# Rotating the tile order of the second hop, running it two half steps ahead, and turning round the edge order of the second relation layer in a graph network kernel

## The reference, cut to what matters

```python
# block 3: two hops, then a product
for _ in range(K_HOPS):
    msg = segment_sum(norm[:, None] * h[src], dst)
    h = (1.0 - ALPHA) * msg + ALPHA * x
return relu(h) @ W.T + b
# block 4: two layers, each with 8 relations
xt = einsum('ni,rio->rno', x, W)             # 8 products of 256x256 for each node
msg = relu(xt[edge_type, src] + b)           # one row for each edge
return segment_sum(msg, dst)
```

## Time and profile before

| What | us |
|---|---|
| median of three executions | 2688.56 |
| the profiled execution, its own time | 2689.72 |
| its span, first to last instruction | 2687.9 |
| last hop-two tile done alone, first gather of layer one | 1507 to 1511 |
| last gather starts | 2675.07 |

### The profile page before, as it was taken

The page is one execution under the profiler, slowest core; times in us unless marked ns, Lnnn a source line. Parts: engine busy times, 40 slices in busy tenths (PEclk is TensorE's granted clock), DMA queues, the critical chain, the costliest instruction groups (busy, mean ns, idle before and its releaser), DMA issues.

```text
span 2687.9 us, 41486 instructions
## 1 busy us (share of the span) xinstructions
PE 2387.7 (89%) x11183; PEld 1798.7 (67%) x11184; DVE 1336.4 (50%) x2819; ACT 572.3 (21%) x1718; POOL 1620.1 (60%) x1701
## 2 busy tenths in 40 slices
PE   7799999999699999999999799998799798766666
PEld 4589999999456588888777477775455555544444
DVE  6788888888676721112373334443344334322232
ACT  1366666666000000000111101111122022000000
POOL 5777777720057777777100377664675757777776
PEclk9899999999799999999999999999899899887887
DMA  3033333322366688553443456653565455333443
GB/s 111 22 118 112 115 115 115 115 114 113 117 191 188 185 315 277 159 180 110 165 148 115 159 161 193 183 159 95 166 184 159 128 154 179 109 103 104 121 120 102
DMA packets 203201, 388.37 MB, mean 144 GB/s; under 512 B 52864, under 2 KB 136942, under 8 KB 202890
## 3 DMA queue, kind: packets, MB, share of 16 engines
q1 hardware_dynamic: 52356, 180.31, 20.0%
q0 software_dynamic: 66944, 111.48, 15.7%
q10 hardware_dynamic: 83718, 94.32, 10.3%
HBM read 244.89 MB, written 141.08 MB: 144 GB/s over the span
## 4 chain that ended last, share of the span: by engine, by line
PE 71%; DVE 10%; issue 8%; POOL 5%; DVEq 2%; ACT 2%; DMA 1%; PEldq 0%; SPq 0%; POOLq 0%; PEld 0%; ACTq 0%
PE agg L1045 16%; PE agg L1166 14%; PE y L922 13%; PE agg L986 9%; PE y L963 5%; POOL gathered L819 5%; PE y L1045 4%; PE agg L1041 4%; PE prod L907 2%; PE y L966 1%; DMA gathered<-table_rel,idx_rel 1%; ACT gathered L1295 1%; DVE onehot L1983 1%; PE y L865 1%; PE turn_ps L892 1%
## 5 line engine op out<-in xcount | busy, mean ns | idle before, releaser
L819 POOL DMA_INDIRECT gathered<-table_rel,idx_rel x840 | 809.4, 964 | 580.4 <-ACTq L1411 258.2
L1166 PE MATMUL agg<-gathered,onehot 128*128 x2072 | 577.3, 435 | 192.4 <-DVE onehot L1983 113.6
L1166 PEld LDWEIGHTS agg<-gathered,onehot 128*128 128x128 f32 x2072 | 434.6, 218 | 328.5 <-issue 262.8
L1983 DVE SCALAR_TENSOR_TENSOR onehot<-iota,keybase,edges 128x256 f32<-128x256 f32 x518 | 240.9, 484 | 642.7 <-PE agg L1166 542.5
L803 POOL DMA_INDIRECT edges_parted<-stream x416 | 402.3, 967 | 179.9 <-issue 126.5
L764 POOL DMA_INDIRECT edges_bucketed<-edges,stream x416 | 401.4, 965 | 148.7 <-issue 122.6
L986 PE MATMUL agg<-h_sb,stream 128*128 128x257 f32 x1250 | 334.9, 392 | 0.0
L1045 PE MATMUL agg<-gathered,stream 128*128 128x256 f32 x1250 | 271.7, 381 | 0.0
L1045 PEld LDWEIGHTS agg<-gathered,stream 128*128 128x128 f32 x1250 | 239.2, 191 | 32.6
L963 PE MATMUL y<-gathered,rel_sb 128*128 128x128 f32 x1300 | 234.8, 290 | 12.6 <-ACT gathered L1295 11.2
L963 PEld LDWEIGHTS y<-gathered,rel_sb 128*128 128x128 f32 x1300 | 218.2, 192 | 36.2 <-ACT gathered L1295 14.4
(11 more groups left out here) (209 smaller groups left out, 2405.3 us busy)
## 6 DMA issues: line engine op xcount, KB each, us to landing
table_rel<-rel_sb ACTq DMA_DIRECT2D x200, 256.0 KB, 3.1
stream<-weights_dense SPq DMA_DIRECT2D x41, 832.0 KB
stream<-weights_dense SPq DMA_DIRECT2D x41, 768.0 KB
weights_dense<-stream SPq DMA_DIRECT2D x25, 832.0 KB, 3.4
stream<-counts_dense SPq DMA_DIRECT2D x50, 416.0 KB
table_rel<-zeros ACTq DMA_DIRECT2D x16, 1280.0 KB
weights_dense<-stream SPq DMA_DIRECT2D x25, 768.0 KB, 3.2
stream<-counts_dense SPq DMA_DIRECT2D x50, 384.0 KB
```

Source lines behind the costliest of these rows:

```text
L819: pool.indirect_dma_start(gathered[:, slot * D:(slot + 1) * D], None, tables[n], bass.IndirectOffsetOnAxis(ap=idx_rel[:, c:c + 1], axis=0) ...
L1166: mm = pe.matmul(agg[b][:, 0:D], onehot[:, place * 2 + k, :], gathered[:, bass.ds(((p + pairs0) & (GP - 1)) * (2 * D) + k * D, D)], start= ...
L1983: nc.vector.scalar_tensor_tensor(onehot[:, place * 2:place * 2 + 2, :], iota[:].unsqueeze(1).broadcast_to([P, 2, P]), keybase[:, bass.ds(t ...
```

## The change

The second hop takes its tiles in the order 10 to 24, then 0 to 9 (`real_tile`); everything in it that reads a tile's block row, scale, rows or residual does so by the real number. So the 15 tiles that are done first are 10 to 24, and the edges of the first pass of layer one are those from tiles 10 to 24; `rel1b` takes those from tiles 0 to 9. Inside `rel1a` the half steps run two ahead: three of them in front of tile 0, then one for each tile.

Layer two takes the parts the other way round. `rel2a` has the edges from tiles 0 to 9, `rel2b` those from 10 to 24, so only ten layer-two products have to be made in `rel1b` (in front of tiles 3 to 12) and fifteen in `rel2a` (three ahead, then in front of tiles 1 to 12). For that, the parted edges are written twice, one copy behind the other, into a new DRAM tensor, and read back from an offset of `late` quads into `kept2`, in the space of the hop's first block row; a second list of indices and of bounds is worked out. POOL waits for that list before layer two. The zeroed rows are tiles 0 to 9 in table one (as many as before) and 10 to 24 in table two (15 instead of 10).

```diff
+    LATE = TILES - EARLY
...
-        def step_at(i):
-            return STEPS[(i + 1) // 2], (i + 1) % 2
+        def steps_with(t):
+            halves = range(3) if t == 0 else (t + 2,)
+            return [(EARLY + h // 2, h % 2) for h in halves]
...
+        LATE_EDGES = {"rel1a": 0, "rel1b": 1, "rel2a": 1, "rel2b": 0}
+        FIRST_KEY = {"rel1a": 0, "rel1b": TILES, "rel2a": 0, "rel2b": TILES + 1}
+        MADE = {"rel1a": 0, "rel1b": TILES, "rel2a": VISITS, "rel2b": VISITS + TILES - 1}
-        PRODUCTS = {"hop2": (0, range(TILES)), "rel1b": (1, range(EARLY)), "rel2a": (1, range(EARLY, TILES))}
+        PRODUCTS = {"hop2": (0, range(TILES)), "rel1b": (1, range(LATE)), "rel2a": (1, range(LATE, TILES))}
...
         def real_tile(n, t):
-            return t + EARLY if n == "rel2a" else t
+            if n == "hop2":
+                return (t + LATE) % TILES
+            return t + LATE if n == "rel2a" else t
...
+                    if n == "hop2" and t == 7:
+                        sp.wait_ge(s_kept, 16)
+                        for k in range(2):
+                            sp.dma_start(parted_twice[:, k * RC:(k + 1) * RC, :], kept).then_inc(s_kept, 16)
...
             pool.wait_ge(s_keys, 1)
             for pi, n in enumerate(RELS):
+                if pi == 1:
+                    pool.wait_ge(s_keys, 2)
...
-                            bass.IndirectOffsetOnAxis(ap=idx_rel[:, c:c + 1], axis=0)
+                            bass.IndirectOffsetOnAxis(ap=(idx_rel[:], idx_rel2)[pi][:, c:c + 1], axis=0)
...
-                     "rel1a": [(-1, lambda t, b: hop2_step(*step_at(t - 1)), range(TILES))],
+                     "rel1a": [(-1, lambda t, b: hop2_steps(t), range(TILES))],
...
-                          (4, lambda t, b: allow(TILES + EARLY, 0, late), range(EARLY - 1, EARLY))],
+                          (4, lambda t, b: allow(TILES + LATE, late, RQ), range(LATE - 1, LATE))],
...
-            for n in RELS:
+            for n, tiles in zip(RELS, (range(LATE), range(LATE, TILES))):
                 for r in range(REL):
-                    late_rows = tables[n][r * NPAD + EARLY * P:(r + 1) * NPAD].rearrange("(p c) d -> p c d", p=P)
-                    act.dma_start(late_rows, zeros[:].unsqueeze(1).broadcast_to([P, TILES - EARLY, D])).then_inc(s_zeroed, 16)
+                    rows = tables[n][r * NPAD + tiles.start * P:r * NPAD + tiles.stop * P].rearrange("(p c) d -> p c d", p=P)
+                    act.dma_start(rows, zeros[:].unsqueeze(1).broadcast_to([P, len(tiles), D])).then_inc(s_zeroed, 16)
...
             load_relations(act, rel_w1, 0, REL, s_wrel[1])
+            act.wait_ge(sum_ready, TILES * (DENSE.index("hop2") + 2))
+            act.wait_ge(s_kept, 16 * 3)
+            act.dma_start(kept2, parted_twice[:, bass.ds(late * QUAD, RC), :]).then_inc(s_kept, 16)
             allow(TILES, late, RQ)
-            over_tiles(act, None, parts["rel1b"], 0)
-            over_tiles(act, None, parts["rel2a"], 0)
-            allow(2 * TILES, late, RQ)
+            over_tiles(act, None, parts["rel1b"])
+            over_tiles(act, None, parts["rel2a"])
+            allow(2 * TILES, 0, late)
...
-                nc.vector.tensor_scalar(early, edges[:, :, 0], float(EARLY * P), None, ALU.is_lt).then_inc(s_early, 1)
+                nc.vector.tensor_scalar(early, edges[:, :, 0], float(LATE * P), None, ALU.is_ge).then_inc(s_early, 1)
...
                 step(nc.vector.memset(key_bounds[near, KEYS:KEYS + 1], RP - 1))
+                step(nc.vector.tensor_scalar(turned_by[near, 0:1], late_at[near, 1:2], -2.0, None, ALU.mult))
...
+                step(nc.vector.tensor_copy(key_bounds2[near, :], key_groups2[near, :]))
...
             for n in PASSES:
+                if n == "rel1b":
+                    dve.wait_ge(s_kept, 16 * 4)
+                    nc.vector.tensor_copy(idx_rel2, kept2[:, :, 1]).then_inc(s_keys, 1)
```

More of the change, by code:

```diff
@@ L471, in static_tiles, with over_tiles @@
                 behind(i)
-        def step_at(i):
-            return STEPS[(i + 1) // 2], (i + 1) % 2
+        def steps_with(t):
+            halves = range(3) if t == 0 else (t + 2,)
+            return [(EARLY + h // 2, h % 2) for h in halves]
         def late_tile(t):
             return EARLY <= t < TILES
-        def over_tiles(eng, visits, parts, first_key, after=(), unrolled=False):
+        def over_tiles(eng, visits, parts, n=None, after=(), unrolled=False):
             all_parts = (*parts, *after)
@@ L568, in staged_rows @@
         def staged_rows(n, bank):
-            at = (bank + (EARLY if n == "rel2a" else 0)) % 2 * KB
+            at = (bank + (LATE if n == "rel2a" else 0)) % 2 * KB
             return turned[:, at:at + KB, :]
@@ L610, in load_late_blocks @@
                 eng.wait_ge((half_free, sum_ready)[part], TILES * (DENSE.index("hop2") + 1) + t)
-                eng.dma_start(half(0, part), dense(w_dram, t, part)).then_inc(s_stream[0][part], 16)
+                eng.dma_start(half(0, part), dense(w_dram, real_tile("hop2", t), part)).then_inc(s_stream[0][part], 16)
         @block.sync
@@ L722, in _ @@
         def _(pool):
-            for k, value in enumerate((NPAD - 1, int(PAD_DST), REL - 1)):
+            for k, value in enumerate((0, int(PAD_DST), REL - 1)):
                 nc.gpsimd.memset(flat_i[:, (k + 1) * F - P:(k + 1) * F], value).then_inc(s_fill, 1)
@@ L911, in relations @@
                 if n == "hop2":
-                    rows = kept_rows(t)
+                    rows = kept_rows(real_tile(n, t))
                 else:
@@ L1139, in hop2_step, with hop2_steps @@
                     rows_product("hop2", s - 1, columns(hopw_t))
+            def hop2_steps(t):
+                for s, half_ in steps_with(t):
+                    hop2_step(s, half_)
             parts = {"hop1": [],
@@ L1157, in visits_of @@
             def visits_of(n):
-                layer, late, tiles0 = PASSES.index(n) // 2, PASSES.index(n) % 2, PASSES.index(n) * TILES
-                pairs0, made0 = layer * RP, layer * VISITS + late * TILES
+                tiles0 = PASSES.index(n) * TILES
+                pairs0, made0 = PASSES.index(n) // 2 * RP, MADE[n]
                 def visit(p, t, b, place, first=False):
@@ L1190, in _ @@
                     pe.sem_inc(S[n, "turned_copied"], 1)
-                if n == "rel2a":
+                if n in ("rel2a", "rel2b"):
                     pe.drain().then_inc(ring_free, 1)
-                over_tiles(pe, visits_of(n), parts[n], TILES * (PASSES.index(n) % 2), unrolled=n == "rel1a")
+                over_tiles(pe, visits_of(n), parts[n], n, unrolled=n == "rel1a")
         @block.scalar
@@ L1864, in hop @@
                     rows_free(n, t)
-                step(nc.vector.tensor_tensor(post[:, 0:D], sums(n, t)[:, 0:D], table(n, t), ALU.add))
+                r = real_tile(n, t)
+                step(nc.vector.tensor_tensor(post[:, 0:D], sums(n, t)[:, 0:D], table(n, r), ALU.add))
                 dve.sem_inc(freed, 1)
@@ L1868, in hop @@
                     step(nc.vector.tensor_scalar(ht(t), ht(t), 0.5, None, ALU.mult))
-                step(nc.vector.scalar_tensor_tensor(post[:, 0:D], post[:, 0:D], half_d(t), ht(t), ALU.mult, ALU.add))
+                step(nc.vector.scalar_tensor_tensor(post[:, 0:D], post[:, 0:D], half_d(r), ht(r), ALU.mult, ALU.add))
             def hop1_rows(t, b):
@@ L1974, in visits_of @@
             def visits_of(n):
-                layer, late = PASSES.index(n) // 2, PASSES.index(n) % 2
-                free0 = layer * VISITS + late * TILES
+                pairs = kept_pairs if n in PASSES[:2] else kept2_pairs
+                free0 = MADE[n]
                 def visit(p, t, place):
```

66 lines of the change are left out of this document (43 added, 23 removed).

## The result

The changed kernel took 2672.58 us (median of 8 executions, 2668.16 to 2677.47), the kernel before 2684.82 us (8 executions, 2681.72 to 2694.28) beside it. The ratio is 0.9948, 95% interval [0.9936, 0.996]: 12 to 14 us less, where the prediction had 9.1 us less and a time of 2679.5. The profiled execution took 2668.16 us, the lowest of the eight and 4.4 us under their median; its span is 2666.3 us.

The account below looks back on a forecast made before the run. PE was taken as the bound up to about 1507 us, then POOL's gathers at 1.271 us plus holds. Holds going from 97 to 88 us gave -9.1 us, so 2679.5 us, range 2662 to 2696.

Parts of the forecast that it names:

- Start of rel1a: From PE's first half step to the first product of rel1a: fewer visits, less idle, better clock; product at 1571, bounds 1566 to 1589.
- Products of rel1a: First to last product of rel1a: 274.7 us before, 1.4 less now; last product at 1844.3, gather 248 at 1856.7.
- the early start is lost again: Rival at the start of rel1a: third half step waits, clock stays low, first product 7 to 8 us later; 2687, chance 0.18.
- End of rel1a: Behind rel1a's last product: 16 visits instead of 3, PE leaves at 1870, index cast 1 us, first layer-two product at 1898.
- Visit-only tiles of rel1b: Tiles of rel1b without products: five more at 8.2 us each, +40 us, so rel2a's first product starts at 2120.
- Gather 452: POOL reaches gather 452 by 2116 and the ring holds it until rel2a's third visit, about 2145: 29 us where 13.9 stood.
- rel2a: Product before tile 1 at 2146.7, then twelve turns of 12.0 or 11.0 us: 140 us, bounds 138 to 148; products done at 2286.7.
- the slower rival: Turns of rel2a stay 13.5 us, set by the chain of product, bias and store: +22 us, 2702; chance 0.10.
- The rest: From gather 540: 299 gathers at 1.271 us are 380.0, plus 1.5; last gather at 2666.0, end of span 2678.8.
- The much faster rival: Visit-only tiles of rel1b go at POOL's pace, so rel1b ends at 2082, 35 us before the sum's 2117: 2645; chance 0.10.
- Edits at no cost: Table two's extra zeroing (up to 16 us uncovered), list stores (at most 5), DVE instructions (at most 2): hidden, cost 0.
- The clock rule: Rule against the change: waits lower the clock in rel1b's visit-only tiles, worst case 3.6 us more for each of 13: 2726; chance 0.02.

Follow-up runs that it names:

- the second chip: The changed kernel, unaltered, on another chip where the kernel before takes 2689 us; its profiled execution took 2677.94 us, the highest of its six.

## Why the prediction was right, and where its terms were off

The forecast case came true: faster, by way of the holds. The profiled execution is the fastest of its eight, and the kernel before took 3.7 us less beside it than in the three executions that the sum starts from, so the terms below come out some us better than in the medians. Almost all of them err to the same side. Point by point, in span times.

- *Start of rel1a.* First product forecast at 1571, measured 1569.53. The stretch has 5.2 us idle (63.00 - 57.84) where I let 5 stay, and the clock went from 0.91 to 0.95.
- *Products of rel1a.* Last product forecast at 1844.3, measured 1841.28; gather 248 forecast at 1856.7, measured 1855.47. The rival that the early start is lost again (0.18) falls, and the second chip, with 1855.79, agrees.
- *The hold at gather 248* I put at some 10 us and it is 1.77. The release was right; POOL was later than I had it (gather 247 at 1852.76, not near 1847), because the ring held it tile by tile. The error costs nothing, since the next gather starts at the release either way.
- *End of rel1a.* First layer-two product forecast at 1898, measured 1894.21; 3.0 of these 3.8 us were there at the last product of rel1a.
- *rel1b with products.* Nine turns forecast at 107.7 us, measured 106.71 (1894.21 to 2000.92).
- *Visit-only tiles of rel1b: the term that was mis-sized.* Tenth product to first of rel2a: forecast 114.3 us (the 74.2 of before and 40 for five more tiles), measured 105.65, which is 8.7 us less. I carried the time of a tile over and counted neither its visits nor its clock. These stretches run from the end of the last product of rel1b to the last turn before rel2a: before, the half steps alone, the changed kernel, the changed kernel on the second chip.

```profile
2088.51:2154.59 66.08, 47.24 (x164) 35.09 (x162) 21.10 (x45) 5.87 (x13) 48.22 (x50) 0.85 0.42 117
...
2069.66:2132.39 62.73, 43.80 (x164) 32.38 (x162) 21.09 (x45) 5.88 (x13) 45.46 (x48) 0.89 0.42 118
...
2007.89:2105.30 97.41, 67.17 (x246) 48.61 (x244) 30.62 (x67) 7.63 (x18) 70.85 (x75) 0.89 0.38 112
...
2008.61:2109.50 100.89, 71.24 (x246) 51.86 (x244) 30.73 (x67) 7.64 (x18) 72.65 (x76) 0.85 0.38 110
```

PE idles 2.3 to 2.4 us a tile in all four. The 8 tiles of before have 36 visits (4.5 each), the 13 tiles now 54 (4.2 each). At the clock of before (0.85) the second chip took 109.13 us from the tenth product to rel2a: so some 5.2 of the 8.7 us go with the visits, an estimate that fits 4.5 visits fewer than thirteen tiles of 4.5 would have, at 1.13 us for a visit by itself. The other 3.5 (109.13 - 105.65) go with the clock, 0.89 for 0.85 with the same 246 matmuls. The half steps alone show the clock by itself: 70.84 us where the same 8 tiles took 74.2. The prediction's sentence that tiles with 4.2 visits take PE 8.2 us read the row of tiles with 4.5. This term is the largest part of the 12.4 us by which the last gather came earlier than forecast.
- *Gather 452.* I forecast a hold of 29 us and the row has 13.16. Its release is the third visit of rel2a, which came 13.4 us earlier (first product 2106.57 instead of 2120), 8.7 of them by the term above. The mechanism was right and the size fell with that term.
- *rel2a.* First product to the one before tile 1: forecast 26.7, measured 26.15. Twelve turns to the end of the visits behind the last one: forecast 140, measured 139.9 (2132.72 to 2272.61). Turns with 5 visits took 11.8 to 12.2 us, none 13.1. That ends the slower rival: the 13.5 us of before were its six visits, not the chain of product, bias and store. The wait on DVE's bias add is in the rows still, at 0.35 to 0.78 us. More than that it doesn't add to a turn, and turns with 4 visits are shorter (10.9 to 11.3 us). The prediction's 11.9 and 11.0 for PE's rows alone should read 11.6 and 10.7 by its own terms (7.1 and 4.5, and a visit less).
- *The rest.* Gather 540 forecast at 2284.5, measured 2272.09. The last gather forecast at 2666.0, measured 2653.62, with 12.7 us behind it.
- *The much faster rival* falls too: gather 419, the last of layer one, starts at 2077.64, and rel1b ends 29 us behind it. PE is busy 67.17 of the 97.41 us there, and the longest of its waits, 13.4 us in all, are for DVE's one-hots; none names a landed gather.
- *Edits at no cost.* The zeroing lasts longer, 106.86 us for the 16 issues instead of 85.57, and moves 369 GB/s. That is 21 us more where the prediction had 16. PE is still busy 60.00 of 60 us. DVE's cast of the second list takes 0.38 us where I took 1. Hop two alone and the first gather (1509.65, 1510.52 on the second chip, 1511.36 before) haven't moved for the worse.

*The clock rule.* In the visit-only tiles the mean clock was 0.89 and 0.85 and never the worst case that the prediction priced at 3.6 us a tile, 2726 in all. Within one kernel it explains the spread: the rows above have PE busy for 67.17 us and for 71.24 with the same matmuls, and idle for 30.2 and 29.7. The Trainium skill, TensorE: Matmul & The Clock Gate, section on HAM oscillation, says that waits inside a loop let the clock fall again and again. The trace agrees in part, as it did before: the clock falls again and again, but not every group is slow. In the changed kernel 20 matmuls at 2029.20 take 4.63 us, near their 4.48 behind a product, and 16 at 2045.03 take 5.21.

What I left out is the price of the two parts apart, though the sum held it. By its own numbers the hold up to gather 248 was to be 1856.7 - 1511.4 - 315.2 = 30 us, 24 less than before, and the total 88. So the holds behind gather 248 were to be 58 us where 43 stood: a loss of 15 us behind the gain of 24. Measured they are 47, a loss of 4, and the half steps alone have as much of it (47.6). The prediction never asked what the turned order brings by itself, and its own sum had the means to.

## What to carry to other kernels

When a producer with a constant pitch sets the end, keep a ledger of what it was held for, stretch by stretch. An edit that moves work between stretches shows as one entry down and another up, and only the sum counts. Price the parts of a combined change apart before the whole: here one part was worth 19 us and the other cost 5. And a tile's duration is not a constant. Count the work in it (here visits: 4.5 or 4.2 a tile) before it is carried over, and let its bounds hold the clock of the new stretch.

## What the runs showed of the hardware that was not expected

- The same instructions run at two speeds on chips of one type: 2687 to 2689 us on two of the chips used and 4062 to 4075 us on four, with the other engines' busy times alike to 1.2%. PE's "issue" time is the largest difference seen (477.4 us at one line that has none on the other kind); the cause is open. A ratio measured on one kind doesn't carry to the other: 1.0018 and 0.9929 for one kernel.
- The same 246 matmuls, with the same idle time among them to 0.6 us, got a mean granted clock of 0.89 in one execution and 0.85 in another. That was worth 3.5 us (109.13 - 105.65) in a stretch of thirteen tiles.
- With the DMA engines' share at 1.05, as the profile counts it, and 369 GB/s, PE's sums lose nothing: 60.00 of 60 us busy with 280 matmuls, as many as at 0.94 and 325 GB/s.
